# Hop 0 on x itself with its first weights applied to the sums, two chunks alternating, and a norm spread over more items

## What is computed

```python
# layer 0
h = relu(A @ (x @ W1) + b1)
h = relu(A @ (h @ W2) + b2)
x = layernorm(x + h)
# layer 1
x = layernorm(x + (A @ x @ V1 + (A @ A) @ x @ V2 + (A @ A @ A) @ x @ V3) / 3)
```

## Time and profile before

| | us |
|---|---|
| median of 3 runs (265.1 to 265.4) | 265.28 |
| the profiled execution, its own time | 265.36 |
| its span, first to last instruction | 263.6 |

### The profile page before, as it was taken

The page is one execution under the profiler, slowest core; times in us unless marked ns, Lnnn a source line. Parts: engine busy times, 40 slices in busy tenths (PEclk is TensorE's granted clock), DMA queues, the critical chain, the costliest instruction groups (busy, mean ns, idle before and its releaser), DMA issues.

```text
span 263.6 us, 3710 instructions
## 1 busy us (share of the span) xinstructions
PE 250.9 (95%) x1146; PEld 201.7 (77%) x1146; DVE 198.1 (75%) x382; ACT 190.8 (72%) x336; POOL 13.6 (5%) x23
## 2 busy tenths in 40 slices
PE   7899999999999999999999999999999999999990
PEld 6566888888886768686888888888888888878760
DVE  0759998896886959595878687867777777776945
ACT  3649887887768686858777878777686867686850
POOL 1000000000002011020000000000000000202022
PEclk9999999999999999999999999999999999999997
DMA  7999999700000000000000000000000000010111
GB/s 244 346 403 405 404 404 406 312 0 0 0 2 1 1 0 2 0 0 0 1 4 0 0 0 2 0 0 0 5 0 0 0 2 0 0 40 2 42 40 41
DMA packets 11252, 20.49 MB, mean 78 GB/s; under 512 B 1248, under 2 KB 2144, under 8 KB 11104
## 3 DMA queue, kind: packets, MB, share of 16 engines
q1 hardware_dynamic: 11088, 19.99, 20.2%
q10 hardware_dynamic: 144, 0.26, 0.3%
HBM read 19.20 MB, written 1.05 MB: 77 GB/s over the span
## 4 chain that ended last, share of the span: by engine, by line
PE 68%; DVE 12%; ACT 7%; issue 6%; POOL 4%; POOLq 0%; DVEq 0%; ACTq 0%
PE filters L345 13%; PE filters L338 12%; PE filters L339 12%; PE pair L345 8%; PE pair L338 8%; PE pair L339 8%; DVE ring_low L557 6%; POOL rstd L264 3%; ACT nodes L422 3%; PE weighted L313 3%; ACT ring_high L462 3%; DVE stats L491 2%; PE turned L355 1%; PE turned L315 1%; DVE operand_low L518 1%
## 5 line engine op out<-in xcount | busy, mean ns | idle before, releaser
L557 DVE TENSOR_TENSOR ring_low<-adj,ring_high 128x512 fp32r<-128x512 f32 x240 | 157.4, 688 | 46.1 <-ACT ring_high L462 45.9
L462 ACT ACTIVATE ring_high<-adj 128x512 fp32r<-128x512 f32 x240 | 146.7, 628 | 32.9 <-PE filters L339 17.2
L338 PE MATMUL filters<-ring_high,operand_low 128*128 128x512 f32 x156 | 62.6, 401 | 1.2 <-DVE operand_low L518 1.2
L345 PE MATMUL filters<-ring_low,operand_high 128*128 128x512 f32 x156 | 61.9, 397 | 0.9 <-DVE ring_low L557 0.5
L339 PE MATMUL filters<-ring_high,operand_high 128*128 128x512 f32 x156 | 60.9, 390 | 0.0
L345 PEld LDWEIGHTS filters<-ring_low,operand_high 128*128 128x128 f32 x156 | 29.3, 188 | 10.8 <-DVE ring_low L557 4.7
L338 PEld LDWEIGHTS filters<-ring_high,operand_low 128*128 128x128 f32 x156 | 29.3, 188 | 7.3 <-DVE operand_low L518 1.4
L345 PE MATMUL pair<-ring_low,operand_high 128*128 128x512 f32 x84 | 33.4, 398 | 0.7 <-DVE ring_low L557 0.5
L339 PEld LDWEIGHTS filters<-ring_high,operand_high 128*128 128x128 f32 x156 | 29.4, 188 | 5.5
L338 PE MATMUL pair<-ring_high,operand_low 128*128 128x512 f32 x84 | 33.4, 398 | 0.0
L339 PE MATMUL pair<-ring_high,operand_high 128*128 128x512 f32 x84 | 32.7, 390 | 0.0
(11 more groups left out here) (67 smaller groups left out, 204.1 us busy)
## 6 DMA issues: line engine op xcount, KB each, us to landing
adj<-a_t SPq DMA_DIRECT2D x47, 256.0 KB, 9.1
resident_raw<-a_t SPq DMA_DIRECT2D x16, 256.0 KB, 9.1
nodes<-x_rows SPq DMA_DIRECT2D x1, 1024.0 KB, 11.2
lead<-lead_in SPq DMA_DIRECT2D x3, 256.0 KB, 5.9
out_rows<-nodes SPq DMA_DIRECT2D x3, 256.0 KB, 2.4
adj<-a_t ACTq DMA_DIRECT2D x1, 256.0 KB, 3.3
out_rows<-nodes SPq DMA_DIRECT2D x2, 128.0 KB, 2.0
lead<-lead_in SPq DMA_DIRECT2D x1, 192.0 KB, 3.3
```

The source lines that it names most:

```text
L338: nc.tensor.matmul(bank, y_low, a_high, start=first, stop=False)
L345: used = nc.tensor.matmul(bank, y_high, a_low, start=False, stop=last)
L462: nc.scalar.activation(ring_high[:, n % RING, :], source, ACT.Copy).then_inc(high_ready, 1)
L557: nc.vector.tensor_tensor(ring_low[:, n % RING, :], source, ring_high[:, n % RING, :].bitcast(F32), ALU.subtract).then_inc(low_ready, 1)
```

## The change

Hop 0 works on x instead of x @ W1: its operand is x rounded out of `nodes`, which is now loaded first, in the five groups. The sums A x of a chunk go through the ring as a wide item with W1 as the operand, into a bank of `pair`; that bank is evacuated with bias and relu, and the post with W2 comes six steps after the wide item. So hop 0 has four wide items and `first_products`, `lead` and its waits are gone. `lifts` has W1 too and comes in two loads, each rounded in its own place.

The tile order changes: in hop 0 chunks 0 and 1 alternate by groups of four tiles; in hop 1, chunk 1's first 8 tiles come ahead of chunk 0's last four. SP's loads follow the new order of hop 0, and each waits for the landing of the one 16 before.

The norm of hops 1 and 4 is spread: statistics in two halves at 1 and 2, moments at 3, the four applications at 6, 7, 8 and 9, the operand at 10 and 11 (in the counting above). `normalised` counts tiles instead of groups, and the last halves have a semaphore of their own. The warm-up has seven products.

```diff
 WIDE = TILES
+LIFTS = {0: 0, 2: 1, 3: 2}
-WARM = 9
+WARM = 7
+IN_FLIGHT = 16
+AHEAD = {1: 8, 2: 12}
+WIDE_AFTER = {(0, 1): 9, (2, 0): 9, (2, 1): 11}
 def tile_order(hop):
-    if hop != 2:
-        return [(hop, c, k) for c in range(CHUNKS) for k in range(TILES)]
-    early = TILES - TPC
-    order = [(hop, c, k) for c in (0, 1) for k in range(early)]
-    order += [(hop, c, k) for c in (0, 1) for k in range(early, TILES)]
-    return order + [(hop, c, k) for c in (2, 3) for k in range(TILES)]
+    last = [(hop, c, k) for c in (2, 3) for k in range(TILES)]
+    if hop == 0:
+        return [(hop, c, g + t) for g in range(0, TILES, TPC) for c in (0, 1) for t in range(TPC)] + last
+    early, ahead = TILES - TPC, AHEAD.get(hop, 0)
+    order = [(hop, 0, k) for k in range(early)] + [(hop, 1, k) for k in range(ahead)]
+    order += [(hop, 0, k) for k in range(early, TILES)] + [(hop, 1, k) for k in range(ahead, TILES)]
+    return order + last
 def all_steps():
     order = [step for hop in range(HOPS) for step in tile_order(hop)]
-    after = {order.index((hop, c, TILES - 1)) + wide_after(hop, c): (hop, c, WIDE)
-             for hop in (2, 3) for c in range(CHUNKS)}
+    after = {order.index((hop, c, TILES - 1)) + WIDE_AFTER.get((hop, c), 7): (hop, c, WIDE)
+             for hop in LIFTS for c in range(CHUNKS)}
 def post_step(hop, c):
+    if hop == 0:
+        return STEPS.index((hop, c, WIDE)) + 6
     return end_of(hop, c) + (8 if (hop, c) == (2, 1) else 4)
+APPLIED = 6
+LIFT_PARTS = {(0, 2, 0): 1, (1, 2, 0): 2}
+def item_of(hop, c):
+    return BEFORE[STEPS.index((hop, c, WIDE))]
+def evacuations(n):
+    return [(hop, c) for hop in range(HOPS) for c in range(CHUNKS) if (hop, c) != (HOPS - 1, CHUNKS - 1)
+            and (item_of(hop, c) + 1 if hop == 0 else BEFORE[end_of(hop, c)]) + RING == n]
...
         @block.sync
+            load_x(0)
+            load_x(1)
+            tiles = [(c, k) for hop, c, k in tile_order(0)]
+            for n, (c, k) in enumerate(tiles):
+                if n == 0:
+                    continue
+                for g, (first, _) in enumerate(X_GROUPS):
+                    if g > 1 and (c, k) == (0, first):
+                        load_x(g)
+                if n >= IN_FLIGHT:
+                    sp.wait_ge(arrival(*tiles[n - IN_FLIGHT]), 16)
+                load(c, k)
+                if n == 24:
+                    sp.dma_start(lift_raw[:, lift_set(1), :], lifts[:, lift_set(1), :]).then_inc(lifts_in, 16)
+                    sp.dma_start(par[:, W2:V3], params[:, W2:V3]).then_inc(layer_0_in, 16)
+            sp.dma_start(lift_raw[:, lift_set(2), :], lifts[:, lift_set(2), :]).then_inc(lifts_in, 16)
...
         @block.tensor
                 if k == WIDE:
-                    bank = filters[:, c, :]
-                    y_high, y_low = lift_high[:, hop - 2, :], lift_low[:, hop - 2, :]
-                    first, last = hop == 2, False
+                    bank = filters[:, c, :] if hop else pair[:, c % 2, :]
+                    y_high, y_low = lift_high[:, LIFTS[hop], :], lift_low[:, LIFTS[hop], :]
+                    first, last = hop < 3, hop == 0
...
         @block.scalar
+            def norm_apply(hop, c, t):
+                tile = nodes[:, c * TPC + t, :]
+                if t == 0:
+                    act.wait_ge(shift_ready, residuals(hop, c))
+                nc.scalar.activation(tile, tile, ACT.Identity, bias=shift[:, t:t + 1], scale=rstd[:, t:t + 1]
+                                     ).then_inc(normalised, 1)
             def visits(n):
-                for hop, c in chunk_ends(n):
+                for hop, c in evacuations(n):
                     evacuate(hop, c)
...
-                for hop, c in posts(n, 5):
-                    if hop in NORMED:
-                        norm_apply(hop, c)
-                for hop, c in posts(n, 6):
+                for t in range(TPC):
+                    for hop, c in posts(n, APPLIED + t):
+                        if hop in NORMED:
+                            norm_apply(hop, c, t)
+                for hop, c in posts(n, APPLIED + TPC):
                     if hop == 1:
                         operand_tiles(hop, c)
...
         @block.vector
             def visits(n):
...
-                    else:
-                        dve.wait_ge(residual_added, residuals(hop, c))
-                        norm_stats(range(c * TPC, (c + 1) * TPC))
-                for hop, c in posts(n, 2):
+                for half in range(HALVES):
+                    for hop, c in posts(n, 1 + half):
+                        if hop in NORMED:
+                            first = c * TPC + half * half_tiles
+                            dve.wait_ge(residual_added, residuals(hop, c))
+                            norm_stats(range(first, first + half_tiles), half * half_tiles)
+                for hop, c in posts(n, 3):
                     if hop in NORMED:
                         norm_moments(residuals(hop, c) - 1, TPC)
-                for hop, c in posts(n, 7):
+                for hop, c in posts(n, APPLIED + TPC + 1):
                     if hop == 1:
                         operand_tiles(hop, c)
```

183 lines of the change are left out of this document (75 added, 108 removed).

## The result

The changed kernel takes 263.06 us (median of 4 runs, 262.42 to 263.33) against 265.34 (265.1 to 266.1) beside it: a ratio of 0.9906 [0.9879, 0.9933], 2.3 us or 0.9% faster. Forecast were 258.8 and a range from 257.2 to 261.2: the sign was right, the size was not, and the range missed it. The profiled execution of after took 262.42 us, its span 260.6. It is the fastest of its four, so what follows explains 2.94 us between two profiled executions, 0.7 more than the medians differ by. One of the ten executions of a later kernel (h1) took 1409 us and is left out of its time.

A forecast was written before the change was run, and what follows sets the result against it. TensorE was taken as the bound at 0.687 us a tile, missed only in hop 0's chunk 0 and at the norms. From 265.36 us, 1.5 for the head and 5.1 for the norm came off: 258.8 us, range 257.2 to 261.2.

The follow-up runs named there:

- h1: The changed kernel with the norm back in its old places (statistics together, four applications in one visit); 266.67 us, ratio 1.002.
- p1: The changed kernel with its SBUF tensors from byte 1024 instead of 1152; 262.20 us, ratio 0.9854.
- b1: The kernel before with its SBUF tensors from byte 1152 instead of 2048, nothing else; 265.82 us in one run.
- a0: The changed kernel, unchanged, run again beside the other kernels; 262.86 us, ratio 0.9891.
- g2: The changed kernel from byte 1024, each norm's four applications on POOL instead of ScalarE, operand at 8 and 9; 267.15 us, ratio 1.0046.

## What to carry over

When work is spread to later items, follow each engine's queue until the next chunk's copy of the same work has run, not until the spread work is done: an instruction that fits in its own period can be the one ahead of the next period's chain. The same lateness has to be carried on to the last chunk, where no later work hides it. And an address is part of a change: look in the diff for where tensors move, and measure the load rate anew before building on it.

## What the runs showed of the chip that I hadn't expected

- The start address in SBUF sets the load rate: 401 to 407 GB/s from byte 2048 (before) or 1024 (p1), 381 to 396 from 1152 (after, b1), with all else equal. A 2 KB packet takes 84 ns in the first case and 87 in the second (medians from 20 to 50 us). Why wasn't tried.
- In twelve of fourteen profiles a single 16 KB instruction packet among the loads goes with one load that lands 0.4 to 1.6 us late (gaps of 1.0 to 2.3 us for 0.64 to 0.68), at a place that differs between kernels and executions. In two the packet has no such gap.
- A POOL subtraction of two 128x512 tensors takes 1.35 us (1.76 once) and VectorE's two-input instruction beside it lasts as long, 0.69 alone. POOL's one-tensor form with multiply and add on 128x128 takes 0.47 to 0.65 us on average, and that with subtract and multiply and the mean read out of `moments` 1.04; which of the two differences makes that (the operations or the stride of the mean) isn't separated.
- The start of a kernel has a stretch of some 3 us at TensorE's lower level, at 8 to 11 us in after and before 8 us in a0, and the granted clock of the rows shows only the first of the two: at the start the distance between products is the surer reading. In g2 the clock fell for 3 us behind a wait of 1.9 us (granted 0.50 from 101 to 103). Late products of 0.3 to 0.5 us apart, as from 24.99 to 27.57 in after, left it at 2.4 GHz (granted 1.00).
